# The second routing of a fused attention kernel, split between two turns: ranks, positions, gates and scatters a turn later, picks dealt over four units

## What is computed

```python
def _L3_ffn_ref(hidden_states, gate_weight, w1, w2):
    x = hidden_states.reshape(-1, D)
    gate_logits = x @ gate_weight.T
    top_vals, top_idx = jax.lax.top_k(gate_logits, TOP_K)
    routing_w = jax.nn.softmax(top_vals, axis=-1)
    ...
    h_sum = jnp.einsum('tef,te->ef', h, mask.astype(h.dtype))
    ...
    out = jnp.einsum('tk,tkd->td', routing_w, y_mean[top_idx])
```

## Time and profile before

| | us |
|---|---|
| median of three runs | 3974.9 (3970.13 to 3979.83) |
| the profiled execution | 3971.64, its span 3969.8 |
| 13 turns, max16 of turn 1 to max16 of turn 14 | 761.76 |
| max16 of turn 14 to compact of turn 15 | 54.0 |
| compact of turn 15 to that of turn 16 | 41.7 |

### The profile page before, as it was taken

The page is one execution under the profiler, slowest core; times in us unless marked ns, Lnnn a source line. Parts: engine busy times, 40 slices in busy tenths (PEclk is TensorE's granted clock), DMA queues, the critical chain, the costliest instruction groups (busy, mean ns, idle before and its releaser), DMA issues. The chain is left out here.

```text
span 3969.8 us, 73176 instructions
## 1 busy us (share of the span) xinstructions
PE 3058.4 (77%) x21122; PEld 1624.8 (41%) x21123; DVE 2298.5 (58%) x4301; ACT 1534.8 (39%) x3010; POOL 907.4 (23%) x1220
## 2 busy tenths in 40 slices
PE   6768699999999999785999229476676667636998
PEld 3335323333333333363666117344444444422336
DVE  6765487777777766264333226366666666635772
ACT  1105446666666666552111004333333333303440
POOL 0003201010100101162000652224444445440000
PEclk8989889999999999876999559777787788757996
DMA  2004612222212221211111113412222222112114
GB/s 69 0 6 154 172 24 48 44 48 43 43 37 44 48 44 19 62 40 37 41 42 41 39 40 115 110 42 48 59 60 50 61 59 59 41 38 93 52 51 119
DMA packets 212745, 222.41 MB, mean 56 GB/s; under 512 B 34738, under 2 KB 186482, under 8 KB 212466
## 3 DMA queue, kind: packets, MB, share of 16 engines
q1 hardware_dynamic: 195842, 188.99, 19.9%
q0 software_dynamic: 14336, 25.72, 2.3%
q10 hardware_dynamic: 2304, 4.20, 0.3%
HBM read 129.02 MB, written 81.90 MB: 53 GB/s over the span
## 5 line engine op out<-in xcount | busy, mean ns | idle before, releaser
L1480 ACT ACTIVATE attn_exps<-attn_sbank 128x392 f32<-128x392 f32 x1600 | 700.9, 504 | 434.8 <-PE attn_sbank L1403 431.5
L1517 DVE TENSOR_REDUCE attn_mx<-attn_rot 128x1 f32<-128x784 f32 x768 | 709.2, 967 | 273.0 <-PE attn_rot L1416 268.4
L2143 ACT ACTIVATE dil_exps<-dil_sbank 128x512 f32<-128x512 f32 x512 | 293.4, 598 | 611.3 <-PE dil_sbank L2043 608.6
L1403 PE MATMUL attn_sbank<-attn_q,attn_k 99*128 99x392 bf16 x1536 | 448.7, 336 | 34.1 <-issue 21.1
L1416 PE MATMUL attn_rot<-attn_k,attn_q 96*128 96x392 bf16 x1536 | 405.0, 347 | 40.6 <-DMA attn_k<-k_pieces 19.2
L2192 DVE TENSOR_REDUCE dil_mx<-dil_rot 128x4 f32<-128x1024 f32 x256 | 308.9, 1220 | 150.1 <-PE dil_rot L2053 146.6
L1443 PE MATMUL attn_acc<-attn_exps,attn_v 128*32 128x392 f32 x3584 | 356.4, 510 | 0.0
L1403 PEld LDWEIGHTS attn_sbank<-attn_q,attn_k 99*128 99x128 bf16 x1536 | 148.3, 97 | 308.8 <-ACT attn_exps L1480 167.0
L2053 PE MATMUL dil_rot<-dil_k,dil_q 96*128 96x256 bf16 x1024 | 186.6, 314 | 102.2 <-DVE dil_mx L2192 43.7
L3005 PE MATMUL silu_ph<-silu_route_w,silu_xT 128*128 x424 | 238.9, 648 | 21.4 <-issue 12.0
L1053 POOL DMA_INDIRECT silu_rows<-dil_r_xt,dil_r_posi x224 | 212.5, 949 | 63.9 <-issue 63.6
(11 more groups left out here) (394 smaller groups left out, 4981.1 us busy)
## 6 DMA issues: line engine op xcount, KB each, us to landing
attn_q<-q_pieces SPq DMA_DIRECT2D x192, 98.0 KB, 3.3
attn_k<-k_pieces SPq DMA_DIRECT2D x192, 98.0 KB, 4.2
silu_x<-silu_rows SPq DMA_DIRECT2D x212, 64.0 KB
dil_q<-dil_q_pieces SPq DMA_DIRECT2D x192, 66.0 KB
dil_k<-dil_k_pieces SPq DMA_DIRECT2D x192, 66.0 KB
q_pieces<-qkv_piece SPq DMA_DIRECT2D x16, 588.0 KB, 3.1
k_pieces<-qkv_piece SPq DMA_DIRECT2D x16, 588.0 KB, 3.2
v_rows<-qkv_v SPq DMA_DIRECT2D x16, 476.0 KB, 3.8
```

The source lines that it names most:

```text
L1403: ins = nc.tensor.matmul(into[:, 0:HS], k_[t.side][g][:, j, c * P:(c + 1) * P], q[t.side][g][:, j, cols], start=True, stop=True)
L1480: nc.scalar.activation(e_[:, n % NP, :], sbank[(n + t.side) % 3][:, 0:HS], ACT.Exp, scale=A_DIM ** -0.5).then_inc(s_ex, 1)
L1517: nc.vector.tensor_reduce(into, rot[b][:, :, 0:HS], AX.XY, ALU.max).then_inc(s_free, 1)
L2143: nc.scalar.activation(e_[:, k % NP, :], sbank[k % 3][:], ACT.Exp, scale=D_DIM ** -0.5).then_inc(s_ex, 1)
```

## The change

Picks stay in the turn that finishes the image, and all that follows them goes into the next turn.

- `steps` gets a fourth flag `older`. With it (turns 2 to 16) `route_steps(h, 2)` puts in, for image t-2: h1 "ranks", "soft" and "place" 0 to 4 (positions); h2 "place" 5 to 10 (gates); h4 "gate"; h5 "store" (SP's gate store); "scatter" 0 to 13, one each in h2 to h15. In turn 16 the same steps for image 15 follow at the end of h15.
- For image t-1: "add" goes from h8 to h9, behind turn 0. SP's fetch becomes a step of its own, "fetch", at h10. "rows" goes from h10 to h12. The 26 picks go over h12 to h15, seven a unit (the last has five), each group behind that unit's max.
- The fetch loses its wait for the rows copied of the image before. DVE's copy of the rows gets a wait for the places of the image before. The links of picks and places have a semaphore each.

So in SP's list load_v and load 0 (h9, behind "add") come before "fetch" (h10), and "store" comes before turn 0. In POOL's list scatter 10 comes before the square, scatter 11 before the norm. `Pipeline` gets one more kind of turn (turn 1) and counts with it.

The core of the diff:

```diff
@@ Router @@
     def sp_fetch(self, sp, im, s_free, pos):
         sp.wait_ge(s_free, pos + 1)
-        im.wait(sp, self.s_xc, lambda e: e)
         sp.dma_start(self.image[:], src).then_inc(self.s_im, 16)
...
     def dve_rows(self, dve, im, rot):
         im.wait(dve, self.s_xt, lambda e: e)
+        im.wait(dve, self.s_cs, lambda e: self.PLACE_LINKS * e)
...
-    def dve_assign(self, dve, im):
+    def dve_picks(self, dve, im):
-        ch = Links(dve, self.s_ch, self.LINKS * im.e, self.LINKS)
+        ch = Links(dve, self.s_ch, self.PICK_LINKS * im.e, self.PICK_LINKS)
...
+        ch.done()
         yield
+
+    def dve_places(self, dve, im):
+        ch = Links(dve, self.s_cs, self.PLACE_LINKS * im.e, self.PLACE_LINKS)
         yield from self.dve_positions(dve, im, ch)
         yield from self.dve_gates(dve, im, ch)
         ch.done()
@@ dilated_attention @@
-    def assign_at(n):
-        return 11 + n // 13 if n < 26 else 14 if n < 31 else 15
-    def scatter_at(n):
-        return 15 + (n + 1) // 2 if n < 3 else 14 + n
-    def steps(finish, exps, maxima):
+    def route_steps(h, lag):
+        out = []
+        if h == 1:
+            out += [("ranks", lag), ("soft", lag)] + [("place", n, lag) for n in range(5)]
+        if h >= 2:
+            out.append(("scatter", h - 2, lag))
+        if h == 2:
+            out += [("place", n, lag) for n in range(5, 11)]
+        return out + {4: [("gate", lag)], 5: [("store", lag)]}.get(h, [])
+    def steps(finish, exps, maxima, older):
...
+            if older:
+                out += route_steps(h, 2)
             if finish:
-                out += {4: [("compact",)], 6: [("den",)], 8: [("add",)], 10: [("rows",)], 13: [("ranks",)]}.get(h, [])
...
+                out += {4: [("compact",)], 6: [("den",)], 9: [("add",)], 10: [("fetch",)], 12: [("rows",)]}.get(h, [])
+                out += [("pick", n) for n in range(26) if 12 + n // 7 == h]
+            if older and not exps and h == D_HEADS - 1:
+                for n in range(D_HEADS):
+                    out += route_steps(n, 1)
             if exps:
                 out += {7: [("score16",)], 9: [("load", 0)], 11: [("weigh16",)], 15: [("load", 1)]}.get(h, [])
...
                         if x[0] == "add":
-                            router.sp_fetch(sp, image_of(t, x), s_free, pos)
+                            pos_add = pos
                         if x[0] == "gate":
-                            router.sp_gate(sp, image_of(t, x), s_free, pos)
+                            pos_gate = pos
+                        if x[0] == "fetch":
+                            router.sp_fetch(sp, image_of(t, x), s_free, pos_add)
+                        if x[0] == "store":
+                            router.sp_gate(sp, image_of(t, x), s_free, pos_gate)
```

More of the change, by code:

```diff
@@ L645, with __init__ @@
 class Pipeline:
-    def __init__(self, steps, rotate, images):
+    def __init__(self, steps, rotate, images, older=False):
         self.images = images
         self.steps, self.rotate = steps, rotate
-        self.of = {-1: steps(False, False, True), 0: steps(False, True, True), "mid": steps(True, True, True),
-                   images - 1: steps(True, True, False), images: steps(True, False, False)}
+        if older:
+            self.of = {-1: steps(False, False, True, False), 0: steps(False, True, True, False), 1: steps(True, True, True, False),
+                       "mid": steps(True, True, True, True), images - 1: steps(True, True, False, True), images: steps(True, False, False, True)}
+        else:
+            self.of = {-1: steps(False, False, True), 0: steps(False, True, True), "mid": steps(True, True, True),
+                       images - 1: steps(True, True, False), images: steps(True, False, False)}
         count = lambda s: sum(x[0] in rotate for x in s)
@@ L658, in __init__ @@
         self.first.append(self.first[1] + count(self.of[0]))
+        self.first.append(self.first[2] + count(self.of.get(1, self.of["mid"])))
         self.per_turn = count(self.of["mid"])
@@ L663, in base @@
             return self.first[lo + 1]
-        return self.first[2] + self.per_turn * (e - 1) if lo < self.images else self.base(1, e - 1) + sum(
+        if lo == 1:
+            return self.first[2] + self.per_turn * (e - 1)
+        return self.first[3] + self.per_turn * (e - 2) if lo < self.images else self.base(2, e - 1) + sum(
             x[0] in self.rotate for x in self.of[self.images - 1])
@@ L794, in __init__ @@
         self.s_hold = m.sem("r_held")
-        self.s_ch = m.sem("r_chain")
+        self.s_ch = m.sem("r_picks_chain")
+        self.s_cs = m.sem("r_places_chain")
         self.s_sct = [m.sem(f"r_rows_scattered{j}") for j in two]
@@ L799, in __init__ @@
         self.WEIGHTS = 16 * (6 if K == 1 else 5)
-        self.LINKS = (13 if K == 1 else 23) + 1 + 3 * NEWTON
         self.ROOT = 2 + 2 + 3 * NEWTON
-        self.PIECES = (self.ROOT + (8 if K == 1 else 13), self.ROOT + (13 if K == 1 else 24))
+        self.PICKS = self.ROOT + (8 if K == 1 else 13)
+        self.PLACES = 5 if K == 1 else 11
+        self.PICK_LINKS = self.PICKS - 2
+        self.PLACE_LINKS = 4 if K == 1 else 9
     def over(self, t):
@@ L1033, in dve_gate, with dve_stored @@
         return ins
+    def dve_stored(self, dve, im):
+        if im.lo > 0:
+            dve.wait_ge(self.s_gd, 16 * im.e)
     def sp_gate(self, sp, im, s_free, pos):
@@ L1829, in steps @@
         return out
-    pipe = Pipeline(steps, ("max", "max16", "turn", "compact", "den", "score16", "weigh16", "add", "rows", "ranks", "gate"), B)
+    pipe = Pipeline(steps, ("max", "max16", "turn", "compact", "den", "score16", "weigh16", "add", "rows", "ranks", "gate"), B, True)
+    ROUTE_STEPS = ("ranks", "soft", "place", "gate", "store", "scatter")
     def image_of(t, x):
-        late = (x[0] in ("weigh", "take") and x[1] == 3) or x[0] in ("compact", "den", "add", "rows", "assign", "ranks", "soft", "gate")
-        return t.plus(-x[2] if x[0] == "scatter" else -1 if late else 0)
+        late = (x[0] in ("weigh", "take") and x[1] == 3) or x[0] in ("compact", "den", "add", "fetch", "rows", "pick")
+        return t.plus(-x[-1] if x[0] in ROUTE_STEPS else -1 if late else 0)
     def bank_left_by(n):
@@ L1999, in do @@
                             router.pool_square(pool, im)
-                        if x == ("assign", router.ROOT):
+                        if x == ("pick", router.ROOT):
                             router.pool_norm(pool, im)
-                        if x[0] == "scatter" and im.lo >= 0:
+                        if x[0] == "scatter":
                             router.pool_scatter(pool, im, x[1])
@@ L2223, in do @@
                             router.dve_rows(dve, prv, rot[b]).then_inc(s_free, 1)
[L2224 to L2228, removed]
+                            pos_rows, picks = pos, router.dve_picks(dve, prv)
+                        if x[0] == "pick":
                             if x[1] == router.ROOT:
                                 dve.wait_ge(s_free, pos_rows + 1)
-                            if x[1] == router.PIECES[0]:
+                            next(picks)
+                        if x[0] == "ranks":
+                            router.dve_ranks(dve, image_of(t, x), rot[b]).then_inc(s_free, 1)
+                            pos_ranks, places = pos, router.dve_places(dve, image_of(t, x))
+                        if x[0] == "place":
+                            if x[1] == 0:
                                 dve.wait_ge(s_free, pos_ranks + 1)
-                            next(picks)
+                            next(places)
                         if x[0] == "gate":
-                            router.dve_gate(dve, prv, rot[b]).then_inc(s_free, 1)
+                            router.dve_gate(dve, image_of(t, x), rot[b]).then_inc(s_free, 1)
                 pipe.run(dve, do, lead=1)
```

3 lines of the change are left out of this document (removed).

## The result

The changed kernel takes 4083.4 us (median of four runs, 4076.4 to 4087.5), the kernel before 3972.5 (four runs, 3967.7 to 3979.8): ratio 1.0276, interval 1.0252 to 1.0299. It is slower, as forecast, but by 111 us where +22 was forecast, and it lies outside the range of 3935 to 4033. Ratios compare undisturbed runs only; one run of the study, 3978.4 us in the kernel with the fetch first, the shifted pick and the loop written out, was disturbed (mean granted clock 0.80 for 0.87) and is left out of its ratio.

The account below looks back on a forecast made before the run. No engine is full in the 13 dilated turns, so waits bound them. Turns of 17.1 + 15.1 + 29.0 = 61.2 us against 58.6 give +34, the last turns -12: +22 on 3971.6, 3994 us (3997 by the median's scale), range 3935 to 4033.

Parts of the forecast that it names:

- (a): In a turn of the dilated attention, from max16 to T: 17.1 us.
- T: The moment in a turn when the copy of "turn 0" on DVE ends; the fetch's times count from it.
- (b): In a turn, from T to the landing of the image fetch: 15.1 us, bounds T + 12.1 and T + 16.8.
- The K wait: PE's wait at max16 for the K pieces, on average 4.1 us in 10 of 12 turns; claimed to go.
- (c): From the fetch's landing to the next max16, DVE nearly full: 29.0 us, 27 to 30.5.
- the gate chain: Turn 15 drops this (about 9 us) and takes back some 2: 35 us for 41.7.
- SP alone: Rival: the fetch is issued late but passes load 0, landing T + 12.1; turn 58.2 us, total 3958; chance 0.15.
- The clock comes back: Rival: fetch late as forecast, but rows and all that follow run at 1.00; turn 57.3, total 3946 us; chance 0.13.
- Two late loads: Rival: more scatters beside load 0, and load 1 comes after max 3; turn 63.5, total 4027 us; chance 0.12.
- The stall does not come: Rival: the fetch lands by T + 6.2; turn 49.5 us, total 3845; chance 0.10.
- under 58 or over 64: Sign that the prediction is wrong: a turn of the dilated attention takes under 58 or over 64 us.
- Waits of ranks, gate and max16 under 1 us: Sign that the prediction is right: in the dilated turns these three waits are each under 1 us.

Follow-up runs that it names:

- the shifted pick: Pick 13 dealt one unit later, in the changed kernel with the fetch ahead of the loads: 3918.4 us, ratio 0.9857; with turns written out too, 3874.1 us, ratio 0.9747.

## Why the prediction was wrong, step by step

**What held.** (a), max16 to T: 17.1 forecast, 17.2 in the turn shown. (b), T to the landing: 15.1 forecast, 15.5 measured; the fetch starts at T + 9.6 (forecast T + 9.4). PE's stand 9 us forecast, 9.6 measured in the mean, 13 times; in turn 14, without a load 0, it is 0.19. Rows at 0.50 in 5.7 us (5.6); the square exposed by 1.61 (1.7). The K wait is gone. The late fetch carried the direction, and its own size was right: undoing the fetch's place takes back 158 us, and making it alone costs 235.

**What failed: term (c), landing to the next max16.** Forecast 29.0 (27 to 30.5), measured 37.5 in the turn shown. By the rows of max16, the raw copy and the last pick in all 13 turns, the 5.6 us a turn that were missing divide so:

- The stop at the jump back: 2.4. Five turns are 70.8 in the mean, the eight others 64.4, and 6.4 x 5 / 13 = 2.4. Writing the loop out took 42 us off the kernel. The step that failed is the sentence that DVE is nearly full in (c) and its sum of operations. I read DVE row by row and took no price for a pass of the loop. DVE's idle time of 3 to 4 us behind the jump was put down to PE there, and a K wait followed. But the trace of before shows the jump on PE, 2.6 us five times, and the prediction did not use it (waits of PE, turns 1 to 14):

```profile
PE dil_sbank L2043 <- issue: 12.8, 5, 2.8
```

- Stretched links: 1.9. From the raw copy to the last pick 14.6 us for 12.7 (the 1.80 and the 1.03 instead of 0.27 each make 2.3). The prediction took the picks' durations from a turn of before in which the norm fell elsewhere, and said that dealing them costs nothing, since the links are the same. They are, but not their neighbours on POOL. That the 1.9 would come back in after itself was not tried; on the kernel with the fetch first, the shift brought 1.3 in the turns without a stop, and nothing with the loop written out.
- max16 to the raw copy: 40.6 in the mean for 39.2: 1.4, spread over (a), (b) and the rows step.

These are 5.7, and rounding takes 0.1. Together 66.8 - 61.2 = 5.6, and times 13, 73 of the 93 us between forecast and profiled execution.

**The start and the last turns: 20 us more.** Turn 15 was to fall from 41.7 to 35 because "the gate chain" leaves it; it took 43.3. This was an error of accounting. The stretch is from compact to compact, and in after ranks, places and gate of the same image stand at h1 to h4 of the next turn, ahead of its compact. The last row of that chain is still in the stretch, 1.9 us ahead of its end at 3621.89:

```profile
3576.71 1.02 DVE L1041 COPY dil_r_image<-dil_rot 16x448 f32<-16x448 f32 x2 [1.65 <-PE dil_rot L1035]
...
3619.99 1.02 DVE L1041 COPY dil_r_image<-dil_rot 16x448 f32<-16x448 f32 x2 [1.65 <-PE dil_rot L1035]
```

Turn 14 took 52.3 for 49.2. The 7.9 us before turn 1 were not forecast. In the profiles of these kernels turn 1 begins anywhere from 2648 to 2661. Two written-out ones that differ only in the dealing of the picks begin it at 2659.40 and 2648.27, so the 7.9 can't be shown to be a term of the change.

**The fetch's landing: right number, unproven reason.** I took T + 15.1 because load 1's last piece had landed late behind its own kind, and read that as the queue. The fetch on ACT's queue speaks against that reading. In after, at 3014 the DMA engines' busy share has fallen to 0.12, and the image is there at 3015.9, about 2 us behind the traffic's end:

```profile
3012.00:3013.00 1.00, 0.00 (x0) 0.00 (x0) 0.00 (x0) 0.00 (x0) 0.00 (x0) 0.50 0.75 193
...
3014.00:3015.00 1.00, 0.00 (x0) 0.00 (x0) 0.00 (x0) 0.00 (x0) 0.00 (x0) 0.50 0.12 42
```

The Trainium skill ("DMA: Bandwidth & Descriptors", section "Queues, rings and completion order") says besides the ring order, on which the prediction drew, that a DMA engine goes round the queue rows packet by packet, and that the semaphore increment of a DMA lands only after every earlier write of that engine, across its queues. The trace agrees with the first: half of the fetch's 144 packets on ACT's row move beside the load's. Of the second no run here can show more than that the landing stays late, 6.3 us against 7.3 on SP's queue and 2.7 alone.

**The rivals.** *SP alone* (T + 12.1) fell: the landing is T + 15.5. *The clock comes back* fell: the granted clock is 0.50 over the whole of rows. *Two late loads* fell: the K wait is gone, although the time is nearest to its side. *The stall does not come* fell for after, but the kernel with the fetch first is that case: it was priced at 49.5 a turn and is 54.3, and 51.3 written out. The mechanism was right; 3.0 of the difference is the jump back, the same term that I lacked in (c), and for the other 1.8 I have no cause.

**The mark "under 58 or over 64".** A turn took 66.8, and so the text called itself wrong, rightly. "Waits of ranks, gate and max16 under 1 us" failed for the ranks, 38.4 us in eight waits: the five long ones, 5.6 to 7.9 us, are those in which DVE stands in its stop.

**Open.** Why the fetch's packets on ACT's queue stand for a microsecond halfway in some turns; for which engine the instruction packet at the jump is; why turns settle at 51.2 with no engine full (PE 524 of 667 us, DVE 506), whether or not the links are stretched; and the spread ahead of turn 1.

## What to carry to other kernels

When a DMA becomes a step of its own in a list, look at what its issuing queue holds ahead of it and at what is on the DMA engines at that moment. Here a 392 KB fetch that was moved behind twelve small loads cost 158 us. Another queue did not help; an earlier issue did. When a change takes away a wait, ask what else lay under that wait: the jump back of a hardware loop cost nothing while a load was awaited a few steps later, and 42 us afterwards. And a wait that ends on a DMA does not shrink when the engine comes to it earlier: with shorter links DVE's stop only grew. And price a chain with the neighbours that it will have, not with those that it had.

## What the runs showed of the hardware

- Where the loop over the turns jumps back, DVE stands 2.8 to 2.9 us with load 1 held back, and 3.9 to 7.7 us while load 1 is in flight (5.1 to 6.4 in after, 3.9 to 6.2 with the fetch on ACT's queue, 4.3 to 6.3 with the fetch first, 6.7 to 7.7 with shorter links too); written out, it doesn't stand at all. About 2 us before it goes on, a packet runs on a DMA queue named "instruction".
- A 392 KB DMA lands 2.7 us behind its issue when no load is ahead of it (2.7 to 3.1 in before). Issued behind twelve 66 KB DMAs, it lands 7.3 us behind it in the median on their queue (up to 10.0), and 6.3 on ACT's (up to 9.8).
- A DVE operation on 112x112 values from two SBUF tiles takes 0.27 us alone, and 1.80 when it starts at the same time as POOL's norm (3029.40 and 3029.39; the norm takes 1.68). The Trainium skill ("SBUF — State Buffer", section "🔬 SBUF: two separate sides") says that a DVE operation with two SBUF inputs and a GpSimd operation hold a shared pair of ports in turn, the other one standing still. The trace agrees: 1.80 is the norm's 1.68 and a little, and DVE's maxima, which read PSUM, keep their 1.21 to 1.23 beside POOL.
